# Graph convolution kernel: two quads' scatter sums side by side in one PSUM bank, both added in one turn

## What is computed

```
h    = relu(layernorm(x));  xp = h @ lin1
C    = 0.5 * (cos(edge_weight * pi / 10) + 1)
W    = (ssp(edge_attr @ mlp_w1 + mlp_b1) @ mlp_w2 + mlp_b2) * C[:, None]
msg  = xp[src] * W
agg  = segment_sum(msg, dst, num_segments=12500)
out  = x + (ssp(agg @ lin2_w + lin2_b) @ lin_w + lin_b)
```

## Time and profile before

| what | value |
|---|---|
| median of 3 runs | 2117.0 us (2116.61 to 2119.41) |
| the profiled execution | 2117.27 us |
| its span in the trace | 2115.5 us |
| POOL busy | 1589.7 us (75%) |
| PE busy | 1362.2 us (64%) |
| DVE busy | 1061.1 us (50%) |
| ACT busy | 891.1 us (42%) |
| mean granted TensorE clock | 0.808 of full |

### The profile page before, as it was taken

One profiled execution on the slowest core, in us unless ns is written; L12 is line 12 of the kernel. 1 busy time (PEld: TensorE's weight loads), 2 busy tenths in 40 slices (PEclk: granted clock), 3 DMA queues, 4 the chain that ended last, 5 costly groups with the idle time before them and its releaser, 6 DMA issues.

```text
span 2115.5 us, 36718 instructions
## 1 busy us (share of the span) xinstructions
PE 1362.2 (64%) x12647; PEld 1147.5 (54%) x12855; DVE 1061.1 (50%) x3434; ACT 891.1 (42%) x1524; POOL 1589.7 (75%) x1666
## 2 busy tenths in 40 slices
PE   6677956656666566665666656656656656566665
PEld 5566745555555555554555545545555555455554
DVE  7878844444444444444444444444444444444444
ACT  5775733433433434333434334334433343343332
POOL 7777777777777777777777777777777777777775
PEclk9989987888777778778778787788777788877887
DMA  8633423233322332323223333233232332332321
GB/s 303 233 94 88 102 79 86 72 84 82 82 78 77 83 83 77 79 75 87 79 76 86 74 82 85 70 86 80 75 86 70 87 86 69 86 84 71 87 71 47
DMA packets 110174, 189.51 MB, mean 90 GB/s; under 512 B 30737, under 2 KB 57298, under 8 KB 109862
## 3 DMA queue, kind: packets, MB, share of 16 engines
q0 software_dynamic: 53152, 108.91, 19.9%
q1 hardware_dynamic: 56838, 78.23, 13.1%
HBM read 174.22 MB, written 12.80 MB: 88 GB/s over the span
## 4 chain that ended last, share of the span: by engine, by line
POOL 57%; issue 21%; PE 8%; DMA 5%; DVE 4%; ACT 4%; DVEq 1%; SPq 0%; POOLq 0%; ACTq 0%
POOL XG L349 57%; DMA XG<-xp_scratch,IX 4%; PE PW L670 2%; PE PA L683 2%; PE PX L653 2%; DVE XG L556 1%; ACT XG L371 1%; DVEq L535 1%; ACT TB L410 1%; PE PX L614 1%; ACT TB L408 1%; ACT TB L406 1%; PE PW L626 0%; DVE SCR L439 0%; PE PW L667 0%
## 5 line engine op out<-in xcount | busy, mean ns | idle before, releaser
L349 POOL DMA_INDIRECT XG<-xp_scratch,IX x1605 | 1528.9, 953 | 492.1 <-issue 479.6
L556 DVE SCALAR_TENSOR_TENSOR XG<-PW,CC,XG 128x128 f32<-128x128 f32 x1661 | 467.6, 344 | 959.3 <-DMA XG<-xp_scratch,IX 956.6
L670 PE MATMUL PW<-W,TB 128*128 128x128 f32 x3322 | 560.5, 324 | 530.4 <-DVE XG L556 517.0
L406 ACT ACTIVATE TB<-PX 128x512 f32<-128x512 f32 x416 | 243.6, 586 | 1016.5 <-PE PX L653 1016.5
L670 PEld LDWEIGHTS PW<-W,TB 128*128 128x128 f32 x3322 | 556.5, 238 | 20.1 <-issue 0.3
L667 PEld LDWEIGHTS PW<-BPB,ones 128*128 128x128 bf16 x416 | 40.9, 98 | 745.8 <-issue 730.9
L683 PE MATMUL PA<-OH,XG 128*64 128x64 f32 x6644 | 357.5, 265 | 19.9 <-DVE AG L537 17.3
L683 PEld LDWEIGHTS PA<-OH,XG 128*64 128x64 f32 x6644 | 293.8, 171 | 88.2 <-issue 60.2
L410 ACT ACTIVATE TB<-TB,HALF 128x512 f32<-128x512 f32 x416 | 299.8, 721 | 13.6
L653 PE MATMUL PX<-AT,W 51*128 51x256 f32 x1662 | 294.2, 482 | 5.4 <-issue 5.4
L528 DVE SCALAR_TENSOR_TENSOR TB<-PX,TB 128x512 f32<-128x512 f32 x416 | 282.5, 680 | 17.7 <-ACT TB L410 17.5
(11 more groups left out here) (74 smaller groups left out, 447.0 us busy)
## 6 DMA issues: line engine op xcount, KB each, us to landing
AT<-attr_t SPq DMA_DIRECT2D x206, 200.0 KB
XG<-xp_scratch,IX POOLq DMA_INDIRECT x1605
AG<-zero SPq DMA_DIRECT2D x1, 6400.0 KB, 22.7
xp_scratch<-XG SPq DMA_DIRECT2D x24, 256.0 KB, 2.4
XR<-x SPq DMA_DIRECT2D x24, 256.0 KB, 5.3
out<-XR SPq DMA_DIRECT2D x24, 256.0 KB, 4.8
AG<-x SPq DMA_DIRECT2D x11, 512.0 KB, 11.0
XG<-x,IX POOLq DMA_INDIRECT x56
```

The source lines that it names most:

```text
L349: e.indirect_dma_start(XG[q % XG_N][0:p, k * D:(k + 1) * D], None, xp, bass.IndirectOffsetOnAxis(ap=IX[0:p, t0 + k:t0 + k + 1], axis=0)).t ...
L406: e.activation(T[:, 0:w], PX[q % X1_N][:, 0:w], ACT.Abs).then_inc(s_ab, 1)
L556: ins = e.scalar_tensor_tensor(out=G, in0=PW[q % 2][0:p, k * D:(k + 1) * D], scalar=CC[0:p, t0 + k:t0 + k + 1], in1=G, op0=ALU.mult, op1=A ...
L670: ins = e.matmul(P[0:p, k * D:(k + 1) * D], TB[q % TB_N][:, k * TILE:k * TILE + p], W2[:, :], start=False, stop=(k == n - 1), skip_group_c ...
```

## The change

The scatter is done in odd turns only, for quads i-5 and i-4, one after the other. Quad q writes columns 0 to 63 of `PA` if it is even and 64 to 127 if it is odd (`sums(q)`). Only the even quad of a pair waits for `s_ac`. VectorE adds in even turns only, both sums of quads i-6 and i-5, and waits for both scatters ahead of the first. The register read of the node number stands ahead of the wait for the scatter now. `OH` has six buffers instead of three. A block of nodes whose `done_by` is even starts one turn later.

```diff
 def starts(c):
-    return done_by(c) + 6
+    return done_by(c) + (6 if done_by(c) % 2 else 7)
...
-    XG_N, TB_N, X1_N, OH_N = 24, 4, 4, 3
+    XG_N, TB_N, X1_N, OH_N = 24, 4, 4, 6
...
+        def sums(q):
+            return PA[:, q % 2 * WIN:q % 2 * WIN + WIN]
...
-                q = i - 5
-                if 0 <= q < NQ:
-                    e.wait_ge(s_sc, q + 1)
-                    if q:
-                        e.wait_ge(s_ac, q)
-                    base = e.value_load(BI[0:1, q:q + 1], min_val=0, max_val=NODES - 1)
-                    A = AG[:, bass.ds(base, WIN)]
-                    e.tensor_tensor(A, A, PA[:, 0:WIN], ALU.add).then_inc(s_ac, 1)
+                for q in (i - 6, i - 5):
+                    if i % 2 == 0 and 0 <= q < NQ:
+                        base = e.value_load(BI[0:1, q:q + 1], min_val=0, max_val=NODES - 1)
+                        e.wait_ge(s_sc, q + 2 - q % 2)
+                        if q:
+                            e.wait_ge(s_ac, q)
+                        A = AG[:, bass.ds(base, WIN)]
+                        e.tensor_tensor(A, A, sums(q), ALU.add).then_inc(s_ac, 1)
...
-                q = i - 4
-                if 0 <= q < NQ:
-                    t0, n, last = quad(q)
-                    e.wait_ge(s_m, q + 1)
-                    e.wait_ge(s_oh, q + 1)
-                    if q:
-                        e.wait_ge(s_ac, q)
-                    for k in range(n):
-                        p = last if k == n - 1 else TILE
-                        for f in (0, D // 2):
-                            ins = e.matmul(PA[f:f + D // 2, 0:WIN], XG[q % XG_N][0:p, k * D + f:k * D + f + D // 2],
-                                           OH[q % OH_N][0:p, k, :], start=(k == 0), stop=(k == n - 1))
-                    ins.then_inc(s_sc, 1)
+                for q in (i - 5, i - 4):
+                    if i % 2 and 0 <= q < NQ:
+                        t0, n, last = quad(q)
+                        e.wait_ge(s_m, q + 1)
+                        e.wait_ge(s_oh, q + 1)
+                        if q >= 2 and q % 2 == 0:
+                            e.wait_ge(s_ac, q)
+                        for k in range(n):
+                            p = last if k == n - 1 else TILE
+                            for f in (0, D // 2):
+                                ins = e.matmul(sums(q)[f:f + D // 2, :],
+                                               XG[q % XG_N][0:p, k * D + f:k * D + f + D // 2],
+                                               OH[q % OH_N][0:p, k, :], start=(k == 0), stop=(k == n - 1))
+                        ins.then_inc(s_sc, 1)
```

## The result

| | before | changed |
|---|---|---|
| median, 8 runs each | 2117.39 us | 2123.27 us |
| lowest to highest | 2116.23 to 2119.41 us | 2121.46 to 2124.13 us |
| profiled execution, span | 2117.27, 2115.5 us | 2122.98, 2121.0 us |

The ratio is 1.0028, interval [1.0019, 1.0038]: the change costs some 6 us, 0.28%. The forecast was 2119.2 us, "no change", with a range to 2122.0 us. The time lies above it.

A forecast was written before the change was run, and what follows sets the result against it. POOL's gathers, one every 1.25 us, were taken as the bound. Terms of 0 in the first phase, 0 in the beat and +2.2 us at the end turned the median 2117.0 into 2119.2 us, range 2116.0 to 2122.0 us.

The forecast's parts named there:

- POOL's beat is the bound: In the loop, POOL's gathers follow one another every 1.25 us and set the time; 1604 beats make 2005.0 us.
- The end: After quad 414's multiply, block 23's later steps delay the last sums: +2.2 us, weighed over two clock levels.
- the lower clock: Likelier case for TensorE at the end: 6.26 us instead of 3.59, 2.7 more; at full clock 1.3 more.
- both adds: At the end, VectorE's last two sums with the register read between them: 1.43 us.
- The loop costs 0: In the loop, paired scatters, waits and moved blocks are hidden by buffers and POOL's beat: 0 us.
- The other stretches I take to be similar or chance: In the loop, longer gathers away from whole-table work at its start were taken as similar or chance.
- 12 us: The gathers' 2017.1 us less 1604 beats of 1.25 us, put down to gathers that took longer.
- Rival B: VectorE's work decides how many gathers stretch: 4.4 us free to move, 2114.8 or 2123.6 us; chance 0.06.
- Rival C: In the loop, TensorE becomes the bound through added idleness per pair: +93 us, 2212 us; chance 0.03.
- Register read ahead: Could save VectorE about 0.5 us a pair, hidden in the loop except at the end.
- Order of the pairs, six masks: In the loop, scattering in pairs and masks waiting for the scatter of q-6 cost 0 on the path.

The follow-up runs named there:

- a1: The changed kernel run again without edits, at POOL's beat: 2122.98 us, 1.0028 of the kernel before.
- e1b: The kernel before with only the later start of node blocks whose `done_by` is even, at POOL's beat: 2118.54 us, ratio 1.0009.
- c0: The kernel before run again without edits, at POOL's beat: 2119.88 us, ratio 1.0000.
- c6: The changed kernel with block 23 starting in the turn it had before, at POOL's beat: 2126.14 us, 1.0031 of the kernel before.
- e4b: The kernel before with each mask built by four instructions of one SBUF input, at POOL's beat: 2108.5 us, ratio 0.9963.
- c8: The kernel before with four-instruction one-input masks and the register read ahead of the waits, at POOL's beat: 2111.68 us, ratio 0.9959.
- c5: The changed kernel with each mask built by four one-input instructions, at POOL's beat: 2116.02 us, 0.9985 of the kernel before.
- e2b: The changed kernel with the mask put in front of both adds, at POOL's beat: 2121.21 us, 1.0020 of the kernel before.
- e2: The changed kernel with the mask put in front of both adds, in a set with the other pace: 0.9996 of the kernel before.
- e6: The changed kernel with block 23 starting in the turn it had before, in a set with the other pace: 0.9996 of the kernel before.
- e4: The kernel before with each mask built by four one-input instructions, in a set with the other pace: ratio 1.0026.

## Why the prediction was wrong

- *POOL's beat is the bound*: right. In all ten traces of this pace POOL pauses for at most 0.32 us between two gathers, so it waits for nobody.
- *The end*: right in place and mechanism. Forecast at the lower clock 6.26 us, found 6.51 (6.52 in a1). The sum has an error: its 1.43 us for "both adds" is 0.25, 0.96 and one add of 0.22, and there are two adds. With both it is 1.65 (found 1.59), and the whole 6.48. The eight matmuls took 2.74 us instead of 2.54; in the earlier trace rows the clock had risen before their end (0.57 granted, 0.50 here). e1b shows the cause alone: its median is 1.7 us over the kernel before. This was worth +2.9 us in the first pair of profiles, +2.5 to 2.9 with c0, against a term of +2.2.
- *The loop costs 0*: this step failed, the term "0 in the beat". The prediction put the loop at "0, covered by the beat", and asked only whether VectorE comes too late for someone. VectorE's instruction can lengthen the beat itself without anybody waiting for VectorE. The number of stretched gathers grew from 29, 43 and 62 (three traces of before's loop) to 120, 111 and 117 (two of the changed kernel, and c6). What they cost grew from 8.4 us in the mean (4.9, 8.2, 12.1) to 12.5 us (12.4, 11.1, 14.0): +4.1 us. The counts are clear of each other, the sums are not (12.1 against 11.1), so the size is less sure than the direction. With 2.7 for the end this makes 6.8 us, and the medians show 5.9 and 6.2. In the set of a1 and e1b they show 4.4 for the pairs and 1.7 for the end.
- *"The other stretches I take to be similar or chance"*: 4.9 of the "12 us" were gathers that start in a mask. The rest of what lay over the plain beats was 6.0 us before 200 us, nearly all beside whole-table and first-phase work of VectorE.
- *Rival B* named the mechanism and was given 0.06, against the sentence "the mask of every quad runs beside gathers on the beat". That is true of masks that start while a gather runs. The ones that count are those in which a gather starts, and sorting the lengths by what VectorE did at the start would have shown it: 29 of 29 stretched ones in the trace at hand. That its time (2123.6 us) is so near to the 2123.27 measured is luck: its 4.4 us were half of a sum taken as free to move, and no count of meetings stood behind them. Of its two gathers "beside line 511" only the one of 1.74 us starts there; the one of 1.94 us starts while line 507 has 0.76 us left.
- The Trainium skill (SBUF — State Buffer, section on SBUF's two sides) says that a VectorE instruction with two SBUF inputs contends too with a GpSimd instruction that reads SBUF, the one that comes first holding the ports. The traces agree for the masks with two SBUF inputs (412 of 412 above), and the adds and multiplies with an input in PSUM never stretched a gather after 200 us. Two SBUF inputs are not needed, though: the masks with one and the casts with one stretched gathers too, as said under e4b. And one point differs: a gather that started first, with the mask coming in its middle, was not longer, nor was the mask by more than 0.04 us. The prediction took the page to hold for large instructions only.
- *Rival C* (TensorE the bound) did not happen at POOL's beat. *Register read ahead*: 1.24 us at the end (c8 against e4b), not 0.5. *Order of the pairs, six masks*: no separate cost found in traces. Whether the pairs cost something more stays open: c5 leaves 0.5 us for it, or some 4 us, by which plain beat its untraced runs had.

The kernel that beats both is e4b (0.9963) or c8 (0.9959). Their intervals overlap. In the sets with the other pace the kernel of c8 is level with before (1.0002), while that of e4b was 0.26% slower.

## What to carry to other kernels

Where an engine works to a fixed beat and sets the time, ask of every instruction elsewhere not only who waits for it but whether it makes the beat's own instructions longer; sort their durations by what the neighbour was doing when they started. If VectorE and GpSimd's gathers run together, use VectorE instructions that read PSUM where there is a choice (none of those in the loop stretched a gather here), or cut an instruction on SBUF alone into short ones: four of 0.25 us in place of one of 0.42 us took the stretches from between 4.9 and 12.1 us to between 0.7 and 1.3 us. And before work is moved a turn, look for the last turn of the kernel, where nothing covers it.

## What the runs showed that was not expected

The plain gather and its beat have two values: 0.944 and 1.2485 us, or 0.946 and 1.2509 us in the mean, 3.7 us over the loop. Each trace has one throughout. It is not the kernel: before's showed 1.2509, 1.2508 and, in a set with the other pace, 1.2482; the one-input masks with the read ahead 1.2481 and 1.2511. The four traces of a1's set all have the shorter one, and three of the four of c0's set the longer. What chooses was not found. It is as large as most effects here, so one profile of each kernel doesn't settle a difference of 4 us.

What was 0.2 or 0.3% slower at POOL's beat (e2b and c6) was no change in the sets with the other pace (0.9996 for both e2 and e6), and the gain of 0.4% (e4b) was a loss of 0.26% there (e4). The changed kernel itself was not run there. The verdict belongs to the pace as much as to the kernel.
